# A Mamba-style selective scan: GpSimd's products with C taken in two pairs, with TensorE's and ScalarE's steps moved to match

## The reference, cut to what matters

```
xc    = conv(x, 4 taps) + bias;  x_dbl = xc @ xproj.T -> dt (64), B (16), C (16)
u     = clip(xc, -10, 10);       delta = softplus(clip(dt @ dtproj.T + bias) + bias)
h[n]  = exp(delta * A[n]) * h[n] + (delta * u) * B[n]      (a recurrence over t)
y     = sum over n of h[n] * C[n]  +  u * D
out   = ((y_fwd + y_bwd) * silu(z)) @ out_proj.T
```

## Time and profile before

| | us |
|---|---|
| median of 3 runs | 8332.51 |
| lowest and highest run | 8323.34, 8334.0 |
| profiled execution | 8327.64 |
| its span | 8325.9 |
| mean granted clock of TensorE in it | 0.948 of full |

### The profile page before, as it was taken

The page is one execution under the profiler, slowest core; times in us unless marked ns, Lnnn a source line. Parts: engine busy times, 40 slices in busy tenths (PEclk is TensorE's granted clock), DMA queues, the critical chain, the costliest instruction groups (busy, mean ns, idle before and its releaser), DMA issues. The chain is left out here.

```text
span 8325.9 us, 116063 instructions
## 1 busy us (share of the span) xinstructions
PE 7232.1 (87%) x32656; PEld 4473.8 (54%) x32656; DVE 7202.0 (87%) x7790; ACT 5330.5 (64%) x12487; POOL 6737.9 (81%) x2833
## 2 busy tenths in 40 slices
PE   7568989998999899977899899899888987779999
PEld 3243555555555555555555555555555555534444
DVE  6921999999999999999999999999999999934444
ACT  3743777777777777776777777777777776610000
POOL 0612999999999999999999999999999999921110
PEclk9789999999999999988899999999999998889999
DMA  3273232313232323221323232323232322154342
GB/s 86 76 199 135 66 117 69 117 66 117 69 117 66 117 69 117 67 98 43 105 76 127 80 129 75 128 80 127 76 128 81 124 98 82 44 199 139 134 141 75
DMA packets 540822, 843.96 MB, mean 101 GB/s; under 512 B 112576, under 2 KB 260032, under 8 KB 522816
## 3 DMA queue, kind: packets, MB, share of 16 engines
q1 hardware_dynamic: 540224, 837.03, 30.5%
HBM read 583.83 MB, written 253.02 MB: 101 GB/s over the span
## 5 line engine op out<-in xcount | busy, mean ns | idle before, releaser
L1179 POOL TENSOR_TENSOR scan_w<-scan_du,scan_bcast_b 128x2048 f32<-128x2048 f32 x1023 | 4633.4, 4541 | 3.6 <-DMA scan_bcast_b<-bc 3.6
L1231 DVE TENSOR_TENSOR_SCAN scan_h<-scan_da,scan_state,scan_w 128x512 f32<-128x512 f32 x2560 | 3178.7, 1280 | 36.6 <-ACT scan_da L1074 21.3
L1074 ACT ACTIVATE scan_da<-scan_delta,scan_prm 128x512 f32<-128x512 f32 x4096 | 2804.3, 685 | 0.0
L962 PE MATMUL scan_yT<-all_ident,scan_hc 128*128 128x128 f32 x10240 | 1514.7, 279 | 768.1 <-DVE scan_hc L1241 767.5
L962 PEld LDWEIGHTS scan_yT<-all_ident,scan_hc 128*128 128x128 f32 x10240 | 1184.8, 142 | 1447.9 <-DVE scan_hc L1241 1068.5
L1231 DVE TENSOR_TENSOR_SCAN scan_hs<-scan_da,scan_state,scan_w 128x512 f32<-128x512 f32 x1536 | 1906.1, 1265 | 59.4 <-PE scan_in_ps L858 41.0
L836 PE MATMUL scan_in_ps<-scan_hn,scan_win 128*128 128x512 f32 x3840 | 1730.8, 593 | 13.5 <-issue 13.5
L1241 DVE TENSOR_TENSOR scan_hc<-scan_h,scan_bcast_c 128x512 f32<-128x512 f32 x2560 | 1652.5, 678 | 38.4 <-ACT scan_state L1054 36.7
L1188 POOL TENSOR_TENSOR scan_hp<-scan_hs,scan_bcast_c 128x512 f32<-128x512 f32 x1024 | 1306.5, 1276 | 60.0 <-issue 54.1
L836 PEld LDWEIGHTS scan_in_ps<-scan_hn,scan_win 128*128 128x128 f32 x3840 | 693.1, 191 | 714.7 <-issue 714.7
L1054 ACT ACTIVATE scan_state<-scan_h 128x1 f32<-128x1 f32 x2560 | 433.4, 169 | 868.6 <-DVE scan_h L1231 861.3
(11 more groups left out here) (128 smaller groups left out, 6761.9 us busy)
## 6 DMA issues: line engine op xcount, KB each, us to landing
yT<-scan_y_out SPq DMA_DIRECT2D x257, 256.0 KB, 2.0
scan_win<-winx SPq DMA_DIRECT2D x128, 512.0 KB, 3.6
xc<-scan_xc_out SPq DMA_DIRECT2D x256, 256.0 KB, 2.0
scan_xc<-xc SPq DMA_DIRECT2D x256, 256.0 KB, 3.9
scan_bcast_b<-bc SPq DMA_DIRECT2D x64, 1024.0 KB, 8.3
scan_bcast_c<-bc SPq DMA_DIRECT2D x64, 1024.0 KB, 7.7
scan_win<-winz SPq DMA_DIRECT2D x128, 512.0 KB, 4.7
scan_x<-x_pad SPq DMA_DIRECT2D x128, 257.5 KB, 2.6
```

The source lines that it names most:

```text
L962: last = nc.tensor.matmul(yT[:, tb], hc_slot(b, n)[:, tb * P:(tb + 1) * P], ident[:], is_transpose=True, start=(i == 0 and tb == 0), stop= ...
L1074: nc.scalar.activation(da[:, n % 2], delta[:, s], ACT.Exp, scale=decay(b, n)).then_inc(S["exp_done"], 1)
L1179: nc.gpsimd.tensor_tensor(w[:, g], du[:, s].unsqueeze(1).to_broadcast([P, G, T]), bcast_b[:, g * G:(g + 1) * G], ALU.mult).then_inc(S["w_d ...
L1231: nc.vector.tensor_tensor_scan(flip(b, h_slot(b, n)), flip(b, da[:, n % 2]), flip(b, w[:, n // G, n % G]), state_of(b, n), ALU.mult, ALU.a ...
```

## The change

1. GpSimd does its four products with C as two instructions of 128x1024: states 2 and 5 together (pair A), 8 and 11 together (pair B). A pair waits for the later of its two scans. To make the pairs contiguous, `hs` gets 6 buffers, one for each state of PN and TN, so scan 11 no longer waits for the turn of state 4. To make room, `u` and `du` get one buffer instead of two.
2. GpSimd's clip and product for the next unit stand behind `weigh_b(b, 3)` and the diagonals.
3. TensorE transposes the `hp` of pair A at step 11 and those of pair B at step 15 (before: one each at steps 5, 8, 11, 14). The projection of xc moves from step 11 to 12.
4. ScalarE copies y at step 4 (was 2), makes `ud` at step 5 (was 10), and copies the convolution at step 11 (was 10).

```diff
-NHS = 4
+HS = {n: i for i, n in enumerate(PN + TN)}
...
-        delta, u, du = (sc.sb(n, [P, 2, T]) for n in ("delta", "u", "du"))
+        delta, u, du = sc.sb("delta", [P, 2, T]), sc.sb("u", [P, T]), sc.sb("du", [P, T])
...
-        hs, hp = sc.sb("hs", [P, NHS, T]), sc.sb("hp", [P, NP, T])
+        hs, hp = sc.sb("hs", [P, NSN, T]), sc.sb("hp", [P, NP, T])
...
-                return hs[:, (b * NSN + SN.index(n)) % NHS]
+                return hs[:, HS[n]]
...
-        NORMAL = dict(into=(0, 2), diag=1, copy=7, conv=5, xc=10, proj=11)
+        NORMAL = dict(into=(0, 2), diag=1, copy=7, conv=5, xc=11, proj=12)
...
-        POOL_AT = [5, 8, 11, 14]
+        POOL_AT = [11, 11, 15, 15]
...
-                    if n == 2:
+                    if n == 4:
                         yT_copy(b - 1)
...
-                    if n == 10:
+                    if n == 5:
                         act.wait_ge(S["skip_loaded"], 2 * DB * LOAD)
                         act.wait_ge(S["u_done"], b + 1)
                         act.wait_ge(S["yT_copied"], b + 1)
...
-                hold(pool, S["ud_done"], b + 1, S["passed"])
-                nc.gpsimd.tensor_scalar(u[:, s], xc[:, s], 10.0, -10.0, ALU.min, ALU.max).then_inc(S["u_done"], 1)
+                hold(pool, S["ud_done"], b + 2, S["passed"])
+                nc.gpsimd.tensor_scalar(u[:], xc[:, s], 10.0, -10.0, ALU.min, ALU.max).then_inc(S["u_done"], 1)
...
-                n = PN[i]
-                pool.wait_ge(c_loaded[n // G], (b // DB + 1) * LOAD)
-                pool.wait_ge(S["scan_done"], b * NS + (n + 1 + SCR))
-                pool.wait_ge(S["hp_used"], b * NP + i + 1)
-                nc.gpsimd.tensor_tensor(hp[:, i], h_slot(b, n), bcast_c[:, n], ALU.mult).then_inc(S["hp_done"], 1)
+                first, second = PN[i], PN[i + 1]
+                for n in (first, second):
+                    pool.wait_ge(c_loaded[n // G], (b // DB + 1) * LOAD)
+                pool.wait_ge(S["scan_done"], b * NS + (second + 1 + SCR))
+                pool.wait_ge(S["hp_used"], b * NP + i + 2)
+                nc.gpsimd.tensor_tensor(hp[:, i:i + 2], hs[:, HS[first]:HS[first] + 2],
+                                        bcast_c[:, first:second + 1:second - first], ALU.mult
+                                        ).then_inc(S["hp_done"], 2)
...
-                weigh_c(b, 1)
-                if nxt:
-                    scan_input(b + 1)
-                weigh_c(b, 2)
                 if b % DB == 0:
                     for k in range(NTN):
                         make_diagonal(b, k)
                 if nxt:
+                    scan_input(b + 1)
                     weigh_b(b + 1, 0)
-                weigh_c(b, 3)
+                weigh_c(b, 2)
...
-                if n in SN:
-                    g = b * NSN + SN.index(n) - NHS
-                    if g >= 0 and SN[g % NSN] in PN:
-                        dve.wait_ge(S["hp_done"], g // NSN * NP + PN.index(SN[g % NSN]) + 1 + NP)
-                    elif g >= 0:
-                        dve.wait_ge(S["h_turn_mm"], g // NSN * NTN + TN.index(SN[g % NSN]) + 1)
-                else:
+                if n in PN:
+                    dve.wait_ge(S["hp_done"], b * NP + PN.index(n) + 1)
+                elif n in TN and b:
+                    dve.wait_ge(S["h_turn_mm"], (b - 1) * NTN + TN.index(n) + 1)
+                elif n in VN:
                     dve.wait_ge(S["hc_done"], b * NV + VN.index(n) + 1)
```

More of the change, by code:

```diff
@@ L918, in unit @@
                 for n in range(NS):
-                    if n in POOL_AT:
-                        i = POOL_AT.index(n)
+                    for i in range(NP):
+                        if n != POOL_AT[i]:
+                            continue
                         pe.wait_ge(S["hp_done"], b * NP + i + 1 + NP)
@@ L1105, in unit @@
                         act.wait_ge(S["yT_copied"], b + 1)
-                        nc.scalar.activation(ud[:], u[:, s], ACT.Copy,
+                        nc.scalar.activation(ud[:], u[:], ACT.Copy,
                                              scale=skip[:, block_of(b):block_of(b) + 1]).then_inc(S["ud_done"], 1)
@@ L1161, in scan_input @@
                 pool.wait_ge(p_in[s], (b // 2 + 1) * (NPL * LOAD))
-                hold(pool, S["ud_done"], b + 1, S["passed"])
-                nc.gpsimd.tensor_scalar(u[:, s], xc[:, s], 10.0, -10.0, ALU.min, ALU.max).then_inc(S["u_done"], 1)
+                hold(pool, S["ud_done"], b + 2, S["passed"])
+                nc.gpsimd.tensor_scalar(u[:], xc[:, s], 10.0, -10.0, ALU.min, ALU.max).then_inc(S["u_done"], 1)
                 pool.wait_ge(S["u_done"], b + 1)
                 pool.wait_ge(S["delta_done"], b + 1)
-                nc.gpsimd.tensor_tensor(du[:, s], delta[:, s], u[:, s], ALU.mult).then_inc(S["du_done"], 1)
+                nc.gpsimd.tensor_tensor(du[:], delta[:, s], u[:], ALU.mult).then_inc(S["du_done"], 1)
             def weigh_b(b, g, single=False):
-                s = b % 2
                 pool.wait_ge(S["du_done"], b + 1)
@@ L1175, in weigh_b @@
                     for i in range(G):
-                        nc.gpsimd.tensor_tensor(w[:, g, i], du[:, s], bcast_b[:, g * G + i],
+                        nc.gpsimd.tensor_tensor(w[:, g, i], du[:], bcast_b[:, g * G + i],
                                                 ALU.mult).then_inc(S["w_done"], 1)
                 else:
-                    nc.gpsimd.tensor_tensor(w[:, g], du[:, s].unsqueeze(1).to_broadcast([P, G, T]),
+                    nc.gpsimd.tensor_tensor(w[:, g], du[:].unsqueeze(1).to_broadcast([P, G, T]),
                                             bcast_b[:, g * G:(g + 1) * G], ALU.mult).then_inc(S["w_done"], G)
             def weigh_c(b, i):
-                n = PN[i]
-                pool.wait_ge(c_loaded[n // G], (b // DB + 1) * LOAD)
-                pool.wait_ge(S["scan_done"], b * NS + (n + 1 + SCR))
-                pool.wait_ge(S["hp_used"], b * NP + i + 1)
-                nc.gpsimd.tensor_tensor(hp[:, i], h_slot(b, n), bcast_c[:, n], ALU.mult).then_inc(S["hp_done"], 1)
+                first, second = PN[i], PN[i + 1]
[6 more added lines that the diff above has]
+                                        ).then_inc(S["hp_done"], 2)
             def unit(b):
```

## The result

The changed kernel takes 8483.94 us in the median (8476.25 to 8486.95, four runs) against 8333.26 us (8323.34 to 8337.5) for the kernel before on the same chip: a ratio of 1.0183, 95% interval 1.0166 to 1.0199. It is slower by 151 us; the forecast was 8475 us. The profiled execution took 8476.25 us, its span is 8474.4 us.

The account below looks back on a forecast made before the run. VectorE, 24.79 us a unit, was taken as the floor. Units at 25.95 against 25.15 us gave +177 us, units 111 to 127 -36, the last 16 +5, together +146: 8475 us, range 8345 to 8540.

Parts of the forecast that it names:

- What bounds the kernel: Scan stage: VectorE, without a gap in a quiet unit, is the floor at 24.79 us; GpSimd is busy 24.62.
- The rival with GpSimd in the lead: GpSimd or its handovers lead and the eight transposes are hidden: about 8235 us, chance 0.12.
- Eight transposes behind product 14: TensorE's loop to scan 8: 0.88 us against 0.55 us of slack, so scan 8 starts 0.33 us late.
- ScalarE's two copies at 0: Copy of y and `ud`, now ahead of `in_copy`, about 0.6 us each, add 0 beyond the 0.33 us.
- The wait of product 14: In units where TensorE's clock falls to 0.50, product 14 is 0.88 us late; a fall costs 1.24 us.
- One fall in two units: TensorE's clock falls in one unit of two, up from two in five: 0.62 us a unit.
- a longer gap ahead of product 9: TensorE's idle gap there is not shorter, and with the longer gap falls come in one unit of two.
- Chunk ends: New cost per 16-unit chunk: 1.4 us of TensorE waiting for pair B plus 0.55 in the last unit, 0.12 a unit.
- The sum: A unit takes 25.12 + 0.62 + 0.09 + 0.12 = 25.95 us against 25.15: +177 us in 222 units, +146 in all.
- The term of -36: Units 111 to 127, without scan 11's wait, go from 27.3 to some 25.2 us: -36 us in 17 units.
- The rival with a fall in every unit (8610): TensorE's clock falls in every unit, by a rule of how transposes count: 138 us more, about 8610, chance 0.06.

Follow-up runs that it names:

- experiment 6: The changed kernel with each GpSimd pair done as two instructions of 128x512 at the same place: 8469.43 us, ratio 1.0179 to the kernel before.
- experiment 7: The changed kernel with the turn of state 4 made four times over, ahead of product 9: 8357.02 us, ratio 1.0033 to the kernel before.
- experiment 2: The kernel before with the transposes of states 8 and 11 both at TensorE's step 15, behind product 14: 8412.55 us, ratio 1.0103.
- experiment 5: The changed kernel with ScalarE's copy of y back at step 2 and `ud` at step 10: 8486.88 us, ratio 1.0199 to the kernel before.
- experiment 1: The kernel before with state 5's transposes moved from TensorE's step 8 to step 11, behind product 9: 8356.50 us, ratio 1.0031.
- experiment 3: The kernel before with six `hs` buffers, single `u` and `du`, and `ud` at ScalarE's step 5: 8289.92 us, ratio 0.9956.
- experiment 9: The kernel of experiment 3 with the convolution's copy at ScalarE's step 11 and the projection of xc at TensorE's step 12: 8270.99 us, ratio 0.9937.
- experiment 4: The changed kernel with pair A's transposes at TensorE's step 8, ahead of the gap before product 9: 8388.67 us, ratio 1.0071 to the kernel before.
- experiment 11: The kernel of experiment 9 with the turn of state 4 made four times over: 8299.64 us, ratio 0.9965 to the kernel before.

## Why the prediction was right

**What bounds the kernel: right.** VectorE's floor was read from one quiet unit; the shortest unit of all runs takes 24.78 us. GpSimd's 24.62 us busy of 24.79 was no bound: experiment 6 gave it back some 0.3 us a unit and nothing slowed down. The rival with GpSimd in the lead (8235 us) is refuted by this and by the idle time of 238.8 us.

**Eight transposes behind product 14: right.** Forecast 0.33 us at scan 8 in each unit; scan 8's own wait was 0.26 us in a unit that is not behind a fall, and 0.47 in one that is. `in_copy` waited for TensorE, as forecast. Experiment 7 shows the loop without the falls: 25.12 us in a steady unit. From scan 0 to scan 8 it is 11.52 us there and 11.21 before, so all in all scan 8 is 0.31 us late, 0.05 of it from ahead of it. Against the 0.87 us of the transposes this makes the slack 0.56 us, where I had read 0.55. Experiment 2, without ScalarE's moves, has the same 0.31 us; its total was missed by 50 us for the reasons given there.

**ScalarE's two copies at 0: right**, by experiment 5: the 0.05 us that they cost ahead of scan 8 comes off scan 8's own wait, since TensorE is late by more.

**The wait of product 14: right in size, a little low in number.** 0.88 us was forecast and measured, and experiment 1 gives the same from the one move. One fall in two units was forecast; product 14 waited in 129 of the 221 units (0.58), and in 90 of the 168 steady ones (0.54). A steady unit took 25.76 us, 0.64 more than the loop alone, so a fall cost 0.64 / 0.54 = 1.19 us where I had 1.24, and the falls 0.64 us a unit where I had 0.62.

The reason that I gave for more falls, a longer gap ahead of product 9, does not hold. In the backward half the gap did not change and the falls still went from 42 to 66; in the forward half it did get longer, and they went from 40 to 68. The gap is the mean idle time of TensorE ahead of product 9's transposes, in steady units:

| kernel | gap, backward | units with a fall | gap, forward | units with a fall |
|---|---|---|---|---|
| before | 2.20 us | 0.39 | 2.30 us | 0.36 |
| after | 2.19 | 0.59 | 2.83 | 0.59 |
| experiment 1 | 2.52 | 0.41 | 2.72 | 0.41 |
| experiment 2 | 2.03 | 0.51 | 2.03 | 0.46 |
| experiment 3 | 1.45 | 0.04 | 1.92 | 0.33 |
| experiment 7 | 0.88 | 0.02 | 1.52 | 0.04 |

In these runs the halves with gaps of 0.9 to 1.5 us have hardly a fall, and those with 1.9 to 2.8 us have one in a third to six tenths of the units, in no order of the gap. One gap of the forward half after:

```profile
4415.91 0.66 PE L963 MATMUL scan_yT<-all_ident,scan_hc 128*128 128x128 f32 x4 [2.83 <-DVE scan_hc L1239]
```

What moved the number from about 0.4 to 0.6 is not isolated. The unit's length alone does not set it either: experiments 1 and 3 have 0.41 and 0.33 (forward) at about the 25.2 and 25.0 us of a unit, experiment 7 has 0.03 at 25.3. What else does stays open; that the number came near one in two was luck in part.

**Chunk ends: right in size.** I gave 0.12 us a unit for what is new there: 1.4 us a chunk for TensorE's wait for pair B and 0.55 for the last unit, 1.95 together. TensorE comes to that wait at its step 15 of a chunk's first unit, when VectorE is in the second unit already, so the cost is in the second unit's length. These took 27.27 us in the mean against 25.76 of a steady unit, before 25.16 against 25.07: 1.42 us new. The first and the last two units of a chunk add 0.86 us. Together 2.28 us a chunk, 0.14 a unit. In nine of the thirteen second units scan 8 is 0.95 to 1.2 us late. In the other four it is 2.7 us late, as in unit 49: TensorE waits longer there, and the clock falls in that wait, so that the eight transposes behind it take 1.75 us (2073.04 to the turned state at 2074.79) and not 0.87.

```profile
2073.04 1.96 PE L924 MATMUL scan_yT<-all_ident,scan_hp 128*128 128x128 f32 x8 [1.48 <-POOL scan_hp L1189]
...
2086.22 1.28 DVE L1229 TENSOR_TENSOR_SCAN scan_hs<-scan_da,scan_state,scan_w 128x512 f32<-128x512 f32 x1 [2.61 <-ACT scan_da L1075]
```

The idle time shown on the transposes themselves, 14.1 us in the whole run, understates this:

```profile
L924 PE MATMUL scan_yT<-all_ident,scan_hp 128*128 128x128 f32 x4096 | 620.4, 302 | 14.1 <-POOL scan_hp L1189 14.1
```

**The sum: right by its parts.** A unit took 25.12 + 0.64 + 0.10 (chunk ends as before) + 0.14 = 26.00 us, forecast 25.95. Units 2 to 110 and 128 to 239 gave +182 us by the trace (forecast +177), units 111 to 127 -37 (forecast -36), the last ones +4 (forecast +5). By its own terms the sum is 8474 + 4.9 = 8479 us; I said 8475, a slip that changes nothing.

The term of -36 was right by luck in part: I ascribed it to the buffers alone, but experiments 3 and 9 show that the buffers give half of it (27.3 to 26.1 us) and the convolution's copy behind exponential 11 the rest (25.3). I had called that move free of cost and said that it takes a wait off the exponential, without a price.

**The rival with a fall in every unit (8610) did not come.** Experiment 7 speaks against its reason: there the added work in the gap is transposes alone, and the clock stays at 1.00. So in this kernel added transposes did keep the clock up. The Trainium skill ("TensorE: Matmul & The Clock Gate", Part 4: PE-mode transpose) says that the full clock does not engage for transpose-mode work; the measured 1.00 is against that as a general rule. Whether transposes count for less than other matmuls, no run here tells.

## What to carry to other kernels

On an in-order engine, look for what stands between the instruction that it waits for and the instruction that others wait for: eight small matmuls there cost their time past the slack, here 0.87 less 0.56 us, while four of them ahead of that instruction had cost nothing in the quiet units before. Ahead of it is not free in general, though: a longer stretch ahead of product 14 made each fall dearer in experiment 1. Measure that slack from two neighbouring units, one in which the consumer waited and one in which it did not. A change that merges instructions on a busy engine is worth nothing if another engine is the floor: here it freed 99 us of GpSimd's time and no time of the kernel, and the order that it brought with it on TensorE cost far more. Take such a change apart: the buffers, `ud` at step 5 and the convolution's copy at step 11 were a gain of some 52 us, and the rest cost some 205. And when averages leave out a chunk's ends, look at where a late step shows up: it can be one unit behind.

## What the runs showed of the hardware

Idle time of TensorE cost more than work. In the changed kernel a gap of 2.19 us (backward) or 2.83 us (forward) ahead of product 9 let the clock fall to 0.50, mostly for 3.4 us, in six of ten units, and 1.3 us of repeated transposes in that gap brought the kernel's time from 1.018 to 1.003 of the one before, with the clock at 1.00 in the chunk shown. The fall costs at the place where it lands, not where the gap is: behind product 9 it cost 1.19 us in the changed kernel, 0.88 of it at product 14; behind product 14 (experiment 4) it made the unit 26.77 us long instead of 25.12. A closed gap can open another one, as experiment 4 showed, and where the clock is low for other reasons the filling only adds work (experiment 11).
